# Routing's normalised rows and logits made inside the top-32 attention, mask preparation beside its keys

## What is computed

```python
def _L1_xattn_ref(query, mem_state, top_k, ...):      # top_k = 32
    scores = jnp.einsum('btd,bsd->bts', q, k) * scale
    vals, idx = jax.lax.top_k(scores, top_k)
    ...                                               # all but the best 32 keys are masked out
    ctx = jnp.einsum('bts,bsd->btd', jax.nn.softmax(scores, axis=-1), v)
    return ctx @ Wo.T + bo
def _L1_ffn_ref(x, Wg, W1, b1, W2, b2):
    logits = jnp.einsum('btd,dn->btn', x, Wg)
    probs = jax.nn.softmax(logits, axis=-1)
    top1_val, top1_idx = ...                          # best expert of each token
    masked = jnp.where(top1_idx[None, :] == jnp.arange(n)[:, None], top1_val[None, :], -jnp.inf)
    vals, idx = jax.lax.top_k(masked, cap)            # cap = 320 tokens an expert
    xe = x_flat[idx]
    h = jax.nn.gelu(jnp.einsum('ncd,ndh->nch', xe, W1) + b1[:, None, :])
    out = jnp.einsum('nch,nhd->ncd', h, W2) + b2[:, None, :]
    ...
x = x + _L1_xattn_ref(_layernorm(x), ctx_1024, 32, ...)
x = x + _L1_ffn_ref(_layernorm(x), ...)
```

## Time and profile before

| what | us |
|---|---|
| median of 3 runs (1409.69 to 1411.76) | 1411.47 |
| profiled execution, device time | 1411.86 |
| profiled execution, span of its instructions | 1410.0 |
| key preparation, about 433 to 446 | 12 |
| attention over the best keys, about 446 to 561 | 115 |
| routing, about 561 to 712.8 | 152 |

### The profile page before, as it was taken

One profiled execution on the slowest core, in us unless ns is written; L12 is line 12 of the kernel. 1 busy time (PEld: TensorE's weight loads), 2 busy tenths in 40 slices (PEclk: granted clock), 3 DMA queues, 4 the chain that ended last, 5 costly groups with the idle time before them and its releaser, 6 DMA issues. The chain is left out here.

```text
span 1410.0 us, 21638 instructions
## 1 busy us (share of the span) xinstructions
PE 1073.4 (76%) x6380; PEld 792.0 (56%) x6382; DVE 905.2 (64%) x3040; ACT 554.4 (39%) x1111; POOL 423.5 (30%) x463
## 2 busy tenths in 40 slices
PE   4788879999995765675478278857999999568842
PEld 1655669899993443632456155535567767445621
DVE  7777755656654888599822677756444445547768
ACT  2476434444443222232023256531334445446531
POOL 1344100000100111061262844401771457324311
PEclk9799969999997555555579569976999999869975
DMA  8344010000002300204032343200337751044202
GB/s 266 92 124 109 7 30 1 1 2 0 1 1 89 91 0 14 84 0 120 13 97 72 88 122 101 72 2 10 96 120 208 216 165 51 13 127 123 72 3 60
DMA packets 108320, 101.05 MB, mean 72 GB/s; under 512 B 10864, under 2 KB 88048, under 8 KB 107824
## 3 DMA queue, kind: packets, MB, share of 16 engines
q1 hardware_dynamic: 76464, 74.22, 18.5%
q0 software_dynamic: 6400, 12.92, 3.5%
q10 hardware_dynamic: 25344, 12.59, 3.1%
HBM read 62.13 MB, written 37.75 MB: 71 GB/s over the span
## 5 line engine op out<-in xcount | busy, mean ns | idle before, releaser
L858 DVE TENSOR_REDUCE mha_nm<-mha_pS 128x16 f32<-128x1024 f32 x96 | 117.2, 1221 | 25.0 <-PE mha_pS L620 24.8
L798 POOL TENSOR_TENSOR mha_ks<-KS,w_ctx 104x1024 fp32r<-104x1024 f32 (+1 forms) x48 | 90.8, 1893 | 94.7 <-POOLq L100 51.5
L1451 ACT ACTIVATE ffn_hid<-ffn_pH,w_ffn 128x512 f32<-128x512 f32 x128 | 85.5, 688 | 55.2 <-PE ffn_pH L1374 54.5
L741 ACT ACTIVATE XH<-mha_pST 128x1024 f32<-128x1024 f32 x96 | 97.8, 1018 | 10.5 <-PE mha_pST L641 10.4
L620 PE MATMUL mha_pS<-mha_ks,mha_qs 96*128 96x256 f32 (+1 forms) x384 | 79.7, 334 | 26.5 <-DVE mha_nm L858 20.0
L1387 PEld LDWEIGHTS ffn_pE<-W2R,ffn_hid 128*128 128x128 f32 x768 | 94.6, 194 | 4.4 <-issue 0.2
L1563 DVE SCALAR_TENSOR_TENSOR ffn_acc<-ffn_pE,ffn_wt,ffn_acc 128x128 f32<-128x128 f32 x192 | 54.0, 345 | 66.7 <-PE ffn_pE L1387 66.7
L1387 PE MATMUL ffn_pE<-W2R,ffn_hid 128*128 128x128 f32 x768 | 95.2, 278 | 0.0
L620 PEld LDWEIGHTS mha_pS<-mha_ks,mha_qs 96*128 96x128 f32 (+1 forms) x384 | 58.8, 212 | 42.0 <-issue 20.5
L2500 POOL DMA_INDIRECT leaf_rows<-XH,tree_place x64 | 63.2, 987 | 57.5 <-DVE tree_place L2580 38.3
L1479 POOL TENSOR_TENSOR X<-X,ffn_xh 128x512 f32<-128x512 f32 (+1 forms) x8 | 10.3, 1284 | 210.9 <-DVE ffn_xh L1509 210.9
(11 more groups left out here) (525 smaller groups left out, 2852.9 us busy)
## 6 DMA issues: line engine op xcount, KB each, us to landing
mha_qs<-queries SPq DMA_DIRECT2D x72, 256.0 KB, 4.0
tree_leaf<-in_leaves_dram SPq DMA_DIRECT2D x96, 96.5 KB
queries<-mha_qh SPq DMA_DIRECT2D x24, 256.0 KB, 2.1
queries<-mha_ql SPq DMA_DIRECT2D x24, 256.0 KB, 2.5
leaf_rows<-top_none SPq DMA_DIRECT2D x12, 512.0 KB, 6.7
tree_xs<-leaf_rows ACTq DMA_DIRECT2D x24, 256.0 KB, 3.2
leaf_results<-tree_ys ACTq DMA_DIRECT2D x24, 256.0 KB
EW<-in_L_W_dram SPq DMA_DIRECT2D x32, 128.0 KB, 2.6
```

The lines of the kernel that those rows point to most:

```text
L741: act.activation(PT[b % PB][:, CU * i:CU * i + CU, :], pST[:], ACT.Exp, scale=SC).then_inc(s["P"], 1)
L798: pool.tensor_tensor(ks[b % KB][0:K1, :, :, :], kb, hb, ALU.mult).then_inc(s["k"], 1)
L858: dve.tensor_reduce(nm[:, t, :], pS[:], AX.X, ALU.max, negate=True).then_inc(s["nm"], 1)
L1451: act.activation(hid[p % 2][:, c, :], pH[c][:], ACT.Gelu, bias=b).then_inc(s["h"], 1)
```

## The change

In `attention_top` ScalarE takes over `normalise`, as an activation with scale RS and bias NB = -mean*RS, one slot earlier in the pipeline (batch b+3 in slot b). VectorE makes NB once, leaves out the copy to MV, and keeps each batch's mean and variance in a tile of two buffers. New steps follow for each batch: GpSimd makes rs2 and nb2 by eight small operations on 128x2 (`scales`, among them a power), ScalarE makes the normalised rows x2 (`rows`), SP stores them to `core.xd`, TensorE turns them (`turn`), ScalarE moves the result (`rows_evac`), and TensorE makes the logits (`logits`) into a bank that stays for the routing. The pipeline is three slots longer on TensorE and ScalarE. `route_top1` loses its scales, normalising, turning, logits, masks and stores; it reads the rows back from DRAM to XH by eight transfers. The two masks' flags are made in `prep_top`. In the ranking, `ca`, `kp` and a scratch tile are computed by expert and then by tile.

```diff
@@ batch_slots(eng, fn, lag, last=1, first=2): slots 0 to 2*first-1 written out, a loop, the last 2*last written out
 prep_top(core, masks)
+        mask_prep = [mask_parts(core, L, masks[L], st, pk[:, 0, P * (L - 2):P * (L - 2) + P]) for L in (2, 3)]
                 if b % 4 == 3:
                     ins.then_inc(s_w, 1)
+            for on_tensor, _ in mask_prep:
+                on_tensor(pe)
+        @blk.vector
+        def _(dve):
+            for _, on_vector in mask_prep:
+                on_vector(dve)
 attention_top, TensorE's slot, behind scores(b + 2, u)
+                if live(b - 4):
+                    logits(b - 4, u)
+                if live(b - 3):
+                    turn(b - 3, 1 - u)
+            def turn(b, u):
+                need(pe, s["x2"], b + 1)
+                need(pe, s["x2T"], b - 1)
+                for j in range(TB):
+                    ins = pe.transpose(pX2[:, S * u + P * j:S * u + P * j + P], x2[u][:, j, :], ident)
+                ins.then_inc(s["x2Tp"], 1)
+            def logits(b, u):
+                need(pe, s["x2T"], b + 1)
+                for j in range(TB):
+                    ins = pe.matmul(pL[:, bass.ds(N1 * (TB * b + j), N1)], x2T[u][:, P * j:P * j + P], core.w("route", "Wg"), start=True, stop=True)
+                ins.then_inc(s["lg"], 1)
-            batch_slots(pe, slot, 2)
+            batch_slots(pe, slot, 5, first=3)
 ScalarE
+            def normalise(b, u):
+                need(act, s["xTp"], b - 1)
+                for j in range(TB):
+                    t = TB * b + j
+                    ins = act.activation(xh[u][:, j, :], X[:, t, :], ACT.Identity, bias=NB[:, bass.ds(t, 1)], scale=RS[:, bass.ds(t, 1)])
+                ins.then_inc(s["xh"], 1)
+            def rows(b, u):
+                need(act, s["r2"], b + 1)
+                need(act, s["x2Tp"], b - 1)
+                need(act, core.rows_out[u], 8 * (b - u))
+                ...
+                    ins = act.activation(x2[u][:, j, :], X[:, t, :], ACT.Identity, bias=nb2[u][:, j:j + 1], scale=rs2[u][:, j:j + 1])
+            def rows_evac(b, u):
+                need(act, s["x2Tp"], b + 1)
+                need(act, s["lg"], b - 1)
+                act.activation(x2T[u][:], pX2[:, S * u:S * u + S], ACT.Copy).then_inc(s["x2T"], 1)
                     q_evac(b + 2, u)
+                if live(b - 4):
+                    rows_evac(b - 4, u)
+                if live(b - 3):
+                    rows(b - 3, 1 - u)
+                if live(b + 3):
+                    normalise(b + 3, 1 - u)
 SP
+            for b in range(B):
+                sp.wait_ge(s["x2"], b + 1)
+                sp.dma_start(core.xd[S * b:S * b + S, :].rearrange("(t p) d -> p t d", p=P), x2[b % 2][:]).then_inc(core.rows_out[b % 2], 16)
 GpSimd, slot b: the add of bo for batch b, then scales(b - 2)
+                need(pool, s["x2"], b - 1)
+                need_apart(pool, s["fin"], b + 1, s["tick2"])
+                link(pool.tensor_scalar(ve[:], mv[u][:, :, 1], EPS, None, ALU.add))
+                link(pool.tensor_tensor(rs2[u][:], ve[:], halves[:], ALU.pow))
+                ...
+                pool.tensor_scalar(nb2[u][:], nt[:], -1.0, None, ALU.mult).then_inc(s["r2"], 1)
 VectorE
-            def normalise(b, u, tiles=range(TB)):
-                ...
-                if step == 3:
-                    need(dve, s["bn"], 2 * b + 2)
-                    dve.tensor_scalar(MV[:, bass.ds(TB * b, TB), :], mv[:], 1.0, None, ALU.mult)
 route_top1
-            rs_dve(dve)
-            for g in range(NG):
-                for t in range(GT * g, GT * g + GT):
-                    ins = dve.tensor_scalar(XH[:, t, :], X[:, t, :], MV[:, t, 0:1], RS[:, t:t + 1], ALU.subtract, ALU.mult)
-                ins.then_inc(s["xh"], 1)
-            for _, on_vector in mask_prep:
-                on_vector(dve)
-            dve.wait_ge(s["L"], NG)
-            link(dve.tensor_tensor(ca, mv, be(rows[:, 0:N1]), ALU.is_equal))
+            link(dve.tensor_tensor(ca, by_expert(mv), over_tiles(rows[:, 0:N1]), ALU.is_equal))
             ...
-            link(dve.tensor_tensor(ex, ex, ca, ALU.mult))
-            dve.tensor_tensor(kp, kp, ex, ALU.add).then_inc(s["eqr"], 1)
+            link(dve.tensor_tensor(ranked, ranked, ca, ALU.mult))
+            dve.tensor_tensor(kp, kp, ranked, ALU.add).then_inc(s["eqr"], 1)
```

More of the change, by code:

```diff
@@ L991, in _, with batch_slots @@
                     pipeline(True)
-def batch_slots(eng, fn, lag):
+def batch_slots(eng, fn, lag, last=1, first=2):
     fn(0, 0)
     fn(1, 1)
-    fn(2, 0)
-    fn(3, 1)
-    with eng.Fori(2, B // 2 - 1) as i:
+    for b in range(2, 2 * first):
+        fn(b, b % 2)
+    with eng.Fori(first, B // 2 - last) as i:
         fn(2 * i, 0)
         fn(2 * i + 1, 1)
-    for b in range(B - 2, B + lag):
+    for b in range(B - 2 * last, B + lag):
         fn(b, b % 2)
@@ L1012, with prep_top @@
 MARK = -3e38
-def prep_top(core):
+def prep_top(core, masks):
     w = lambda n: core.w("top", n)
@@ L1151, in _ @@
                 q_evac(b, b)
-            batch_slots(act, slot, 2)
+            normalise(2, 0)
+            batch_slots(act, slot, 5, last=2, first=3)
         @blk.sync
@@ L1266, in _ @@
             rs_dve(dve)
-            normalise(0, 0)
-            normalise(1, 1)
-            batch_slots(dve, slot, 2)
+            dve.scalar_tensor_tensor(NB[:], MV[:, :, 0], -1.0, RS[:], ALU.mult, ALU.mult).then_inc(s["nb"], 1)
+            batch_slots(dve, slot, 2, first=3)
 NROT, NE, EH = 4, 6, 256
@@ L1685, in route_top1 @@
         pX = [st.ps(f"pX{u}", [P, 512]) for u in range(2)]
-        pL, pM, pC, pP, pR = (st.ps(n, [P, 512]) for n in ("pL", "pM", "pC", "pP", "pR"))
-        names = "xh xTp xT L own cnt tot thr dx ex mvp MTp rowsp dgr eqr ca prf ones sl xd high piece t1 t2 t3 bw mix same res k kt lo fill v vb of row tok tb".split()
+        pM, pC, pP, pR = (st.ps(n, [P, 512]) for n in ("pM", "pC", "pP", "pR"))
+        names = "own cnt tot thr dx ex mvp MTp rowsp dgr eqr ca prf ones sl back high piece t1 t2 t3 bw mix same res k kt lo fill v vb of row tok tb".split()
         s = {n: st.sem(n) for n in names}
-        rs_act, rs_dve = token_scales(core, st, MV[:, :, 1], RS[:], "a")
-        mask_prep = [mask_parts(core, L, masks[L], st, pC[:, P * (L - 2):P * (L - 2) + P]) for L in (2, 3)]
         halves = [(w1, w2) for w1, w2 in ((core.w1h, core.w1l), (core.w2h, core.w2l))]
@@ L1784, in _ @@
         def _(act):
-            rs_act(act)
-            for g in range(NG):
-                act.wait_ge(s["xTp"], g + 1)
-                if g >= 2:
-                    act.wait_ge(s["L"], g - 1)
-                act.activation(xT[g % 2][:], pX[g % 2][:], ACT.Copy).then_inc(s["xT"], 1)
             act.wait_ge(s["dx"], 1)
@@ L2016, in _ @@
             pool.wait_ge(s["sl"], 1)
-            pool.wait_ge(s["xd"], 16 * NG)
+            for u in range(2):
+                pool.wait_ge(core.rows_out[u], 8 * B)
             for j in range(RING):
@@ L2899, in four_layers @@
                 mask_buffers(core, L, masks[L], stack)
+            with ExitStack() as layer:
+                core.KT[1], core.VWo = sb(layer, "KT1", [P, B * SK]), sb(layer, "VWo", [P, B, P])
+                prep_top(core, masks)
+                core.pL = kept.enter_context(nc.psum_tensor("logits", [P, T * N1], F32))
+                attention_top(core)
             attention_buffers(3, stack)
```

128 lines of the change are left out of this document (67 added, 61 removed).

## The result

The changed kernel took 1391.47 us (median of 4 runs, 1388.74 to 1394.12) against 1411.62 for the kernel before on the same chip: ratio 0.986, 95% interval 0.984 to 0.988. Forecast were 1394.6 and a range of 1385 to 1404. On another chip the same pair gave 1391.16 against 1411.44, ratio 0.986 (0.984 to 0.988).

What follows compares the result with a forecast made beforehand. VectorE was taken to set the attention's pace, TensorE close behind, with a dependent chain fronting routing. Terms -28.1 - 7.0 + 4.9 + 1.5 + 5.2 + 6.6 = -16.9 on the 1411.47 median gave 1394.6 us, range 1385 to 1404.

Steps and rivals of the forecast that it cites:

- A: Front of routing: the logits' reduction starts some 0.6 us in instead of 28.7, -28.1 us.
- rival 4: Front of routing: a step behind the early reduction waits, so it gives 20 instead of 28: 1403 us; chance 0.10.
- B: Ranking in routing: operations along the storage order take 0.69 us each; saving 5.7 to 7.4, taken -7.0 us.
- C: Key preparation: second mask's steps queue behind the first's and are not hidden, +4.9 us, bounds 0.8 and 5.5.
- D: Attention's start: four ScalarE activations ahead of its first copy, NB first, and delayed first exponentials: +1.5 us.
- third pair: Attention's start: ScalarE's third pair of activations delays the first exponentials by another 0.5 us.
- E: Attention's slots: first five at 6.0 us on VectorE's pace, ten at TensorE's 7.2; +5.2 us, bounds -3.2 and +12.
- the bare chain: TensorE's chain of one attention slot without its wait for VectorE's xh: 5.93 us, of 6.29 with 0.36 waiting.
- Rival 1: Attention: TensorE's chain stays hidden, by a clock of 1.0 or loads fitting its waits: 1385.2 us; chance 0.19.
- Rival 2: Attention slots become longer than 7.2 us through ScalarE, run-time addresses or GpSimd; at 7.9, 1401.6 us; chance 0.16.
- F: Attention's end: a new tail of GpSimd operations, activations and store, with TensorE's results about 1 us later: +6.6 us.
- The clock: TensorE in the attention's slots stays at granted clock 0.50; 17.00 us busy at 0.50 in routing spoke against a rise.

Runs made afterwards that it cites:

- e_split: The changed kernel with VectorE's two mask preparations interleaved in key preparation, both first halves ahead of either wait for TensorE's transposes: 1386.07 us, ratio 0.983.
- e_norm_dve: The changed kernel with the normalisation of each batch back on VectorE as in the kernel before: 1388.59 us, ratio to the kernel before 0.986.
- e_fill: The changed kernel with TensorE's two added groups, logits and turn, moved into its waits: 1384.97 us, ratio to the kernel before 0.983.
- e_pow3: The changed kernel with GpSimd's power made three times, same result: one run of 1394.31 us.
- the three edits: The changed kernel with TensorE's added groups in its waits, masks interleaved, and the last two batches' scales shared between GpSimd and VectorE: 1381.81 us, ratio 0.978.
- e_tail: The changed kernel with the last two batches' scales shared: GpSimd makes variance plus eps and the power, VectorE the six operations behind: 1390.80 us, ratio 0.984.
- e_masks: The kernel before with only the two masks' flags moved from routing to key preparation: 1409.08 us against 1408.43, ratio 1.001.
- e_turn2: The changed kernel with each batch's turn made twice on TensorE: 1392.03 us, one run.

## Why the prediction was right, step by step

*A, the front of routing*: -28.26 against -28.1. Nothing became late behind it: the way to the thresholds took 74.56 us against 74.87, and rival 4 fell. The masks' 4.7 us were part of these 28, which the prediction had not set apart.

*B, the ranking*: -6.15, inside its 5.7 to 7.4 but not the -7.0 taken. The step that was mis-sized is "With all of them along the storage order I take 0.69": four operations that read an f32 tile across it took 1.0.

*C, the masks*: +4.54 against +4.9. The mechanism was right, the second mask's comparison and reduction in line behind the first's wait; the fixed cost is 0.35, and e_split shows it.

*D, the start*: +0.50 against +1.5. The four activations ahead of the first copy and NB cost 0.5 where 1.0 had been taken: with them back on VectorE (e_norm_dve) the piece was 7.27 again. The 0.5 of the third pair did not show at all.

*E, the slots*: +5.60 against +5.2. The mechanism was right, but that the number came out so close is in part luck. The ten slots from the sixth on took 71.9 us, 7.19 each, where 7.2 had been worked out from the bare chain and the loads of the earlier trace rows; the first five took 30.6 instead of 30.0. TensorE itself, however, needed 7.20 us from one turn of top_pk to the next only where the slots are written out, as in its sixth:

```profile
494.21 0.63 PE L1116 MATMUL top_pT<-w_ctx,top_pk 128*128 128x128 f32 x2
...
501.41 0.63 PE L1116 MATMUL top_pT<-w_ctx,top_pk 128*128 128x128 f32 x2
```

In the hardware loop behind it the next seven of these turns took until 553.66, 7.46 us each. The added groups are not the reason, they took 1.28 us (522.61 to 523.89) against 1.23 worked out. The step that was mis-sized is "so 0.36 is waiting and the bare chain is 5.93": the prediction let the turn of the input follow 0.8 us behind the product with the values, by the loads, but in the kernel after, where it waits for nobody, its matmuls start 1.01 us behind (525.09 to 526.10). So only 0.15 of the 1.16 us was waiting, and 7.46 less 1.28 gives a bare chain of 6.18 in the loop. What makes a loop slot longer shows in the waits for ScalarE, 0.56, 0.47 and 0.75 us in the slot shown above and 0.47, 0.47 and 0.56 in a written-out one; no run separates the loop's register addresses from the rest. These 0.26 us a slot stayed out of the sum because VectorE still ran ahead: its sixth slot began 3.0 us ahead of TensorE's turn (491.20, 494.21) and its fifteenth 5.2 (555.89, 561.04), so some 2 us of the ten slots came out of that lead. Four experiments show that TensorE's chain sets the slots, and e_fill that it does so only because of where the groups were put. Rival 1 described what would be had if the loads fitted into the waits; it fell as a forecast, and came true as an experiment. Rival 2 fell in its main form: 0.44 us more on ScalarE cost 0.31 in all.

*F, the end*: +7.89 against +6.6. The step that was mis-sized is "eight dependent GpSimd operations, rows of 0.25 and some 0.05 between, 2.4 us". It was 3.41, since the gaps are 0.18 to 0.20 and the power 0.71; and batch 15 waited in line for batch 14, about 1.0 more. Against that, the last statistics came only 0.33 us later behind the last mask step than before (4.23 against 3.90), not 1.0.

*The clock* stayed at 0.50 from 462.5 us to the end of the attention in the kernel after, with TensorE busy 77% of the window of ten slots: the 17 us of the earlier trace rows had been the right witness. They hold turns and narrow products mixed, so they do not show which of the two kept it there.

The errors of B, D and F were of different sign, and all six together come to 1.0. So by its own steps the forecast should have been missed on the slow side, at about 1395.5. The measured gain is 20.1 us (20.3 on the second chip), and the steps give 16.1. The remaining 4 are in no stretch that was forecast, and stay open: the code outside the steps took between 1120.7 and 1134.0 us in the fourteen profiled executions of this study, with no order by what had been changed. Chance alone is not shown either, since the 16.1 lie just outside both intervals (16.5 to 22.7 and 16.8 to 23.1 us). That the time fell 3 us below the forecast is therefore not the doing of any term of the sum.

## What to carry over

Work that moves to an engine with idle time is free only if it is put into that idle time: an engine's list is in order, and with the same two groups behind the scores the sixteen slots took 5.6 us more than before, and with them in the waits further up 2.1 less. Where two chains of the form "prepare, wait for another engine, finish" stand in one list, all preparing goes ahead of the first wait. A short operation on an engine with slow hand-overs is to be priced with its gap, and the last item of a pipeline, where nothing hides it, is to be given to the engine that is then idle.

## What the runs showed of the hardware

**VectorE and GpSimd hold each other up.** VectorE's mask step L1299, with two inputs in SBUF, takes 0.22 us, but in some slots one of its two operations takes 0.80. In the kernel after there are three, at 483.67, 490.27 and 496.94, and each starts within 0.03 us of GpSimd's add of bo. The last:

```profile
496.93 0.72 POOL L1260 TENSOR_TENSOR X<-X,w_top 128x256 f32 x1
496.94 0.80 DVE L1299 SCALAR_TENSOR_TENSOR top_pk<-top_wk,top_pr 128x64 f32<-128x64 f32 x1 [0.23 <-DVE top_wk L1291]
```

It ends 0.09 us behind the add. In the kernel before the two met as well, but the add began first: in fourteen of the sixteen slots one mask operation took 0.37 to 0.46 us, and the mean over all 32 was 0.291 against 0.278 in the changed kernel. What is new are the long ones, which start together with the add. In the slots that TensorE sets this costs nothing; in the fourth and fifth it is the step from 6.0 to 6.6 us, and in e_pow3, where the two did not meet there, these slots took 6.05 and 6.02. With the three edits VectorE sets the pace, and seven of them took 0.75 to 0.80; with TensorE's edit alone (e_fill) it was four. Three more at 0.58 us each are 1.7, and the stretch of the slots was 1.83 longer (102.85 against 101.02). The Trainium skill, "SBUF — State Buffer", "SBUF: two separate sides", says that the two engines share a pair of ports as an exclusive lock which a VectorE operation with two SBUF inputs needs as well against a GpSimd operation that reads SBUF, and that the loser is blocked for the whole instruction; the trace agrees, with 0.58 us lost to an add of 0.72. Moving the add away from the mask step was not tried.

**The clock rose once the waits were filled.** In every kernel that left TensorE's order as it was, the granted clock from 462 to 555 us was 0.50 throughout, with the doubled turn too (busy 56.40 of 72.00 us). In e_fill it was not; rows of 3.4 us each, granted clock ahead of the last two numbers:

```profile
483.00:486.40 3.40, 3.04 (x10) 2.17 (x10) 2.55 (x21) 1.12 (x4) 2.22 (x8) 0.50 0.12 36
486.40:489.80 3.40, 2.00 (x15) 1.65 (x15) 3.05 (x22) 3.02 (x9) 1.29 (x4) 0.92 0.13 39
489.80:493.20 3.40, 2.21 (x14) 1.42 (x13) 2.49 (x16) 2.15 (x6) 1.96 (x7) 1.00 0.01 2
```

It was back at 0.50 some 7 us later, and rose once more for about 3.5; in the kernel with the three edits it rose once, for about as long. The slots there were no shorter (6.97 and 6.19 us), so no gain is put down to it. What made it rise, these runs don't tell: the 17.00 us of the earlier trace rows, busy throughout, were not followed by it, and the clock of that kernel stayed at 0.50 until past 600 us.

**GpSimd's hand-overs differ in length.** In GpSimd's chain of the changed kernel 0.18 us lie between two dependent operations, where an extra increment is issued with each wait (`need_apart`); in e_tail's two operations, with the wait alone, 0.08 (574.20 to 574.28). That the increment is the cause is likely and not shown; over the seven hand-overs of a batch it would be 0.7 us, and a kernel with that alone was not run.

**The rest of the program scatters.** The part of the program behind the experts' loads, the same code in all kernels, took from 688.4 to 698.2 us in the fourteen profiled executions. In e_masks it was 690.9 us at a mean granted clock of 0.86, in the kernel with the three edits 697.8 at 0.84 (a window each: length, busy time of PE, PEld, DVE, ACT, POOL, granted clock):

```profile
708.60:1399.50 690.90, 527.93 (x3232) 371.40 (x3233) 401.98 (x1037) 289.84 (x623) 294.21 (x326) 0.86 0.33 92
```

```profile
683.90:1381.70 697.80, 539.19 (x3233) 379.79 (x3233) 402.52 (x1037) 289.71 (x623) 293.42 (x326) 0.84 0.33 91
```

VectorE's and ScalarE's busy times are equal to 0.2%, TensorE's are 11 us apart, which would fit a scatter that comes from the clock. But e_turn2 took 690.9 us there with TensorE busy 536.5 at 0.84, so the clock alone does not explain it, and the cause stays open. The stretches between seams in which the clock did not change repeated to 0.1 us, which is why the steps above are read from them and not from the medians.
